# Attention loop of a decoder layer: values a step later, weight rounding off GpSimd, thresholds of the context spread out

## What is computed

```python
# attention input and its result ("context"), per chunk of 64 tokens:
ch_bias = (max + min) / 2 per channel;  xz = xp - ch_bias
tmax = max|xz| per chunk;  cmax = max|xz| per chunk and channel
thr = tmax / 2 ** arange(7, -1, -1);  idx = sum(cmax > thr[:7])
scale = tmax / 2 ** (7 - idx) / 7
result = clip(round(xz / scale), -8, 7) * scale
# attention
probs = softmax(Q K^T);  ctx = probs V
# ternary FFN weights
scale = mean|w|;  wq = clip(round(w / scale), -1, 1) * scale
```

## Time and profile before

| what | us |
|---|---|
| median of three runs | 1176.83 (1174.73 to 1180.32) |
| the profiled execution | 1178.66 |
| its span, first to last instruction | 1176.9 |
| first stage, to the first row maximum | about 128 |
| attention loop | about 510 |
| third stage | about 537 |

### The profile page before, as it was taken

The page is one execution under the profiler, slowest core; times in us unless marked ns, Lnnn a source line. Parts: engine busy times, 40 slices in busy tenths (PEclk is TensorE's granted clock), DMA queues, the critical chain, the costliest instruction groups (busy, mean ns, idle before and its releaser), DMA issues. The chain is left out here.

```text
span 1176.9 us, 13444 instructions
## 1 busy us (share of the span) xinstructions
PE 955.5 (81%) x4128; PEld 369.3 (31%) x4128; DVE 863.0 (73%) x1622; ACT 688.4 (58%) x1103; POOL 388.9 (33%) x303
## 2 busy tenths in 40 slices
PE   3667799889998888988887678797989798879465
PEld 1223322222222222222122343343434343434122
DVE  7996688888899989999883658568656765575245
ACT  3778377777777677767564034265526562555255
POOL 4103355656665676653002423130014001400000
PEclk9779699999999999999999879999999899989788
DMA  8966455555556554546334102310251025002500
GB/s 306 350 234 213 163 153 164 170 180 181 182 181 181 163 172 153 177 138 178 92 101 137 56 38 64 80 72 1 58 120 73 1 53 120 7 1 61 118 1 36
DMA packets 90684, 145.00 MB, mean 123 GB/s; under 512 B 12339, under 2 KB 52147, under 8 KB 89078
## 3 DMA queue, kind: packets, MB, share of 16 engines
q1 hardware_dynamic: 90614, 144.16, 40.7%
HBM read 84.75 MB, written 42.21 MB: 108 GB/s over the span
## 5 line engine op out<-in xcount | busy, mean ns | idle before, releaser
L1277 DVE TENSOR_REDUCE neg_max<-banks 128x1 f32<-128x512 f32 x512 | 331.4, 683 | 48.2 <-PE banks L1129 44.7
L1237 ACT ACTIVATE probs<-banks 128x512 f32<-128x512 f32 x512 | 278.3, 600 | 116.3 <-PE banks L1150 115.5
L1129 PE MATMUL banks<-k_st,q_st 96*128 96x512 bf16 x512 | 198.0, 392 | 20.9 <-DVE neg_max L1277 18.4
L1150 PE MATMUL banks<-q_st,k_st 99*128 99x512 bf16 x512 | 195.4, 385 | 13.2 <-ACT probs L1237 9.3
L1164 PE MATMUL banks<-probs,v_st 128*32 128x512 f32 x1024 | 137.1, 607 | 17.5 <-ACT pv_z L1250 16.3
L1543 POOL TENSOR_TENSOR rstd<-vare,half 128x1 f32<-128x1 f32 x48 | 26.8, 558 | 358.7 <-DVE vare L1535 358.7
L1749 PE MATMUL banks<-q_T,f_int_all 128*128 128x512 bf16 x512 | 127.5, 391 | 19.5 <-DVE h_ring L1770 19.4
L1129 PEld LDWEIGHTS banks<-k_st,q_st 96*128 96x128 bf16 x512 | 50.4, 99 | 171.2 <-DVE neg_max L1277 105.3
L1808 PE MATMUL banks<-hz,I_h 128*128 128x512 f32 x128 | 67.9, 667 | 34.5 <-DMA hz<-h_turned 32.1
L1759 DVE TENSOR_TENSOR h_ring<-banks,gate_row 128x512 f32<-128x512 f32 x64 | 44.1, 689 | 60.3 <-PE banks L1749 58.5
L1399 POOL TENSOR_SCALAR woT<-woT 128x1024 f32<-128x1024 f32 x24 | 87.2, 3633 | 2.4 <-ACT woT L1393 0.4
(11 more groups left out here) (263 smaller groups left out, 1519.1 us busy)
## 6 DMA issues: line engine op xcount, KB each, us to landing
hz<-h_turned SPq DMA_DIRECT2D x64, 256.0 KB
f_int_all<-in_ffn_dram SPq DMA_DIRECT2D x24, 512.0 KB, 8.6
qk_parts<-parts SPq DMA_DIRECT2D x32, 384.0 KB, 2.5
q_st<-qk_parts SPq DMA_DIRECT2D x32, 384.0 KB, 3.9
k_st<-qk_parts SPq DMA_DIRECT2D x32, 384.0 KB, 4.9
woT<-in_ffn_dram SPq DMA_DIRECT2D x24, 512.0 KB, 3.4
qk_parts<-parts SPq DMA_DIRECT2D x32, 256.0 KB, 2.9
pv_rows<-pv_z SPq DMA_DIRECT2D x32, 256.0 KB, 5.1
```

Source lines behind the costliest of these rows:

```text
L1129: pe.matmul(s_bank[(16 * g.n + tile) % SB], q_st[g.i][0:KR, j, qt * P:(qt + 1) * P], k_st[g.i][0:KR, j, :], start=True, stop=True).then_in ...
L1150: pe.matmul(st_bank[at % STB], k_st[g.i][:, j, kt * P:(kt + 1) * P], q_st[g.i][:, j, :], start=True, stop=True).then_inc(st_mm, 1)
L1237: act.activation(probs[ktp][:, j, i, :], st_bank[(16 * g.n + 2 * w + i) % STB], ACT.Exp).then_inc(exp_done, 2)
L1277: dve.tensor_reduce(neg_max[:, g.h, tile:tile + 1], s_bank[(16 * g.n + tile) % SB], AX.X, ALU.max, negate=True).then_inc(max_done, 1)
```

## The change

PV_AT goes from steps 1, 2, 6, 7 to 2, 3, 6, 7. An FFN piece is loaded second in SP's period rather than last, clipped by DVE in step 5 of its group (one instruction with two operations), and stored as bf16 by ACT in step 0 of the next group (an activation with bias -MAGIC); POOL has no part in it. The 11 threshold pieces go to steps 1, 3, 5, 7 of r = 0 and steps 1 to 7 of r = 1; POOL's scaling goes from r = 1 to r = 2; ACT's four roundings go from steps 1 to 4 to steps 1, 3, 5, 7 of r = 3; DVE's four finishing operations go from steps 5, 6, 7 of r = 3 and step 0 of r = 4 to step 7 of r = 3, step 0 of r = 4, and steps 1 and 6 of r = 5.

```diff
+        neg_magic = keep("neg_magic", [P, 1])
...
                 def _(pool):
+                    pool.memset(neg_magic[:], -MAGIC)
...
-            PV_AT, QK_AT, V_AT, HIGH_AT, MIDDLE_AT = (1, 2, 6, 7), (3, 5), 5, (4, 6), (5, 7)
+            N_AT = ((3, 7), (4, 0), (5, 1), (5, 6))
+            PV_AT, QK_AT, V_AT, HIGH_AT, MIDDLE_AT = (2, 3, 6, 7), (3, 5), 5, (4, 6), (5, 7)
             def v_bank(kt):
...
                             act_middle(act, g.tile(2), MIDDLE_AT.index(u))
-                    if g.b > 1 and g.r == 3 and 1 <= u <= 4:
-                        act_round(act, g.b - 2, u - 1)
+                    if g.b > 1 and g.r == 3 and u % 2:
+                        act_round(act, g.b - 2, u // 2)
+                    if u == 0 and 0 < g.n <= PIECES:
+                        act_ffn_store(act, g.n - 1)
...
+                    if u == 5 and g.n < PIECES:
+                        dve_ffn(dve, g.n)
             def dve_context(dve, g, u):
...
-                    else:
-                        dve_levels(dve, g.b - 2, u - 1)
-                if g.b > 1 and g.r == 1 and u < 4:
-                    dve_levels(dve, g.b - 2, 7 + u)
-                if g.b > 1 and g.r == 3 and u > 4:
-                    dve_n(dve, g.b - 2, u - 5)
-                if g.b > 1 and g.r == 4 and u == 0:
-                    dve_n(dve, g.b - 2, 3)
+                    if u % 2:
+                        dve_levels(dve, g.b - 2, u // 2)
+                if g.b > 1 and g.r == 1 and u:
+                    dve_levels(dve, g.b - 2, 3 + u)
+                if g.b > 1 and (g.r, u) in N_AT:
+                    dve_n(dve, g.b - 2, N_AT.index((g.r, u)))
...
-                if g.n < PIECES:
-                    pool_ffn(pool, g.n)
                 if g.b and g.r == 7:
-                if g.b > 1 and g.r == 1:
+                if g.b > 1 and g.r == 2:
...
             def sp_period(sp, g):
+                if g.n + 1 < PIECES:
+                    sp_ffn(sp, g.n + 1)
...
-                if g.n + 1 < PIECES:
-                    sp_ffn(sp, g.n + 1)
-                    need(sp, "f_done", 2 * PIECES)
+                    need(sp, "f_done", PIECES)
                     load_wo(sp, woT[:], bo_row[:])
             def sp_ffn(sp, c):
-                need(sp, "f_done", 2 * (c - 1))
+                need(sp, "f_done", c - 1)
             def act_ffn(act, c):
...
-            def pool_ffn(pool, c):
+            def dve_ffn(dve, c):
-                need(pool, "f_round", c + 1)
-                did(pool.tensor_scalar(raw, raw, MAGIC - 1.0, MAGIC + 1.0, ALU.max, ALU.min), "f_done")
-                need(pool, "f_done", 2 * c + 1)
-                did(pool.tensor_scalar(f_int_all[:, c, :], raw, -MAGIC, None, ALU.add), "f_done")
+                need(dve, "f_round", c + 1)
+                did(dve.tensor_scalar(raw, raw, MAGIC - 1.0, MAGIC + 1.0, ALU.max, ALU.min), "f_clip")
+            def act_ffn_store(act, c):
+                need(act, "f_clip", c + 1)
+                did(act.activation(f_int_all[:, c, :], f_ring[:, c % 2, :], ACT.Identity, bias=neg_magic[:]), "f_done")
             def groups(eng, period):
```

## The result

The changed kernel takes 1194.8 us, median of 4 runs, against 1178.6 for the kernel before on the same occasion: a ratio of 1.016 (95% interval 1.011 to 1.022). Forecast was 1164.1 in a range of 1152 to 1176. It is slower where a gain was forecast, and lies above the slower rival's 1187 too.

The account below looks back on a forecast made before the run. PE was taken to bound even groups, DVE and ACT to pace odd ones. Terms -3.5 - 3.4 + 5.5 - 3.8 - 1.4 - 3.2 - 1.0 - 1.4 - 0.5 gave -12.7, so 1164.1 us median, range 1152 to 1176.

Parts of the forecast that it names:

- slower rival: Store on ACT not hidden, 1.1 per even group, with the clip's 1.2; odd groups gain nothing: 1187 us, chance 0.08.
- PV a step later: Steps 1 to 3: PV's wait for pv_z goes; alone -0.5 us for an odd group, nothing for an even one.
- cost C of a plain even group: Net change per plain even group from PV's move, store and clip: +0.5 us, eleven groups +5.5.
- The store on ACT: Step 0, 24 times, ahead of step 1's exponentials: some 0.5 us in an even group, nothing in an odd one.
- the clip: DVE's step 5, 24 times: 0.6 us and a wait of about 0.5 in even groups; odd groups' lighter steps absorb it.
- a clock of 0.91: Group 19: gaps from roundings, a late piece and finishing operations give half speed for 3.4 us; spreading gives -3.2.
- Pieces off POOL, and sooner: About 0.4 us off a plain group's maxima chain; groups 5 and 7 return 1.2 and 0.5 each, -3.4 together.
- Thresholds spread: Groups 16 -2.9, 24 -2.6, 17 +0.9, 25 +0.8: net -3.8 us.
- Scaling, rounding and finishing: Group 18 -1.4 us, 19 -3.2, 27 -1.0, 14 and 22 -0.7 each, 26 to 30 in all -0.5.
- The wait in sp_spread: Group 21: SP waits until step 6 for finishing operations; store of values and sums behind it are needed later: nothing.
- The rule on the shared port: Exclusive lock for a whole instruction would give about 50 us off; the row gives 7 at most, and it decides.

Follow-up runs that it names:

- pv_only: The kernel before with only the values' multiplications moved to steps 2, 3, 6, 7: 1195.2 us, ratio 1.016.
- pv_fill: The kernel before with values in steps 2, 3, 6, 7, plus four unused matmuls on PE in step 1 ahead of the transpose: 1182.0 us, ratio 1.005.
- after_fill: The changed kernel with four unused matmuls added on PE in step 1: 1177.3 us, ratio 1.000.
- ffn_only: The kernel before with only the pieces changed (clipped by DVE, stored by ACT, loaded early): 1166.1 us, ratio 0.992.
- ctx_only: The kernel before with only the context's thresholds, scaling, rounding and finishing at their new steps: 1186.8 us, ratio 1.008.
- pv_back_n_early: The changed kernel with values back in steps 1, 2, 6, 7 and the last finishing operations earlier, at (4, 6) and (5, 1): 1165.0 us, ratio 0.991.
- ffn_clip7: The kernel before with only the pieces changed, and the clip in step 7 instead of 5 in groups 6, 14, 22: 1166.8 us, ratio 0.992.
- pv_split: The kernel before with values in steps 2, 4, 6, 7 of even groups and 2, 3, 6, 7 of odd ones: 1190.6 us, ratio 1.013.

## Why the prediction was wrong

*PV a step later* is the step that failed. I put it at "-0.5 for an odd group and at nothing for an even one". Alone it measured +19.7 us, 18.9 of them between the loop's first and last maximum. Three things were wrong in it, and one more in the cost C of a plain even group that it went into.
- I saw that the transpose would wait for DVE's last part and that step 3 would be 3.1 us, but charged neither. The wait went from 7.7 to 40.8 us; PV in step 1 had been the work that hid it. (In group 4 I also took the start of DVE's last part, 199.62, for its end, 199.79.) The late PV did slip into a gap of the odd groups: in pv_only's groups 9 and 11 step 3 grew by 1.1 and step 5 shrank by as much. But step 1 kept nearly all of its length, idle where PV had been, so they gained 0.3 and 0.2 us, not 0.5, and groups 3 and 13 lost 1.4 and 1.6 to the clock.
- Step 3 of an even group went up by the full 1.1 us of a PV, of which I had charged only a share, and "nothing" for the move alone. Steps 1 and 2 gave back 0.85 (I had 0.6): together +0.3 in pv_only's groups 2 and 4, and up to +1.4 in group 10, where DVE's last part comes later.
- TensorE's clock was in the sum only as a past gain ("a clock of 0.91" in group 19). That idle time at a new place could lose it was not among the terms nor the rivals. It is the largest: pv_fill gives back 13 of the 19.7 us and after_fill 17.
- The store on ACT costs 0.57 in steps 1 and 2 of the changed kernel's groups 2 and 4, near the 0.5 charged (in 8 to 12, where DVE's last part comes later, the waits for it cover most of that), and the clip, of which I had charged a share, costs nothing. So C, put at +0.5, measured +0.8 in groups 2, 4 and 8, +1.0 in 10 and +0.3 in 12: not far off, but from terms of which the largest, step 3, was mis-sized. The other even groups, from 6 to 22, add the clock, or stand among the terms below.

*The slower rival* had 0.08. Its mechanism, the store on ACT (1.16 us, 24 times) ahead of step 1's exponentials, is there, at half its price: 0.57 instead of 1.1, and only together with the values' move; in ffn_only the even groups stay at 14.6. Its clip of 1.2 costs nothing in the plain groups, its loss in the odd groups did not come, and the clock, which it did not have, brought more than both: that its 1187 lies nearest to 1194.8 is in part luck.

*Pieces off POOL, and sooner*: right in sign. Groups 5 and 7 returned 1.8 each (forecast 1.7), odd groups 0.6 to 0.7 (forecast 0.5). But the 0.5 was booked for PV's move and the pieces together and comes from the pieces: ffn_only alone gives 0.4 to 0.6. For each of groups 14 and 22 I forecast -0.7, and it is +3.8 and +3.5: I took GpSimd's relief into account there, not that the clip itself runs into GpSimd's subtraction (1.52), next to c_cmax which does the same.

*Thresholds spread*: 16 gained 2.8 alone (forecast 2.9) and 17 lost 1.5 (0.9). In the whole, 16 lost the gain to a wait of 2.52 for the maxima, to step 3 (4.3 us, PV with projection) and to a half clock, and 17 lost 3.1 with a double one.

*Scaling, rounding and finishing*: for group 19 I forecast -3.2 from spreading them. Without the values' move it did fall, to 15.5, but it does so in ffn_only too, where nothing of them is spread; spread alone, in ctx_only, it grew to 21.4. The gain was GpSimd's relief from the pieces, booked to the wrong part. In the whole it kept 1.0 of it, with a wait of 2.14 for the maxima and a half clock.

*The wait in sp_spread* was named and costed at "nothing", with "the store of values and the sums, needed a group later" behind it. What was left out is that the sums wait in turn for the store to land, about 5 us, and that the next group's maxima's DMA stands behind both: +5.1 in group 30, 8.5 in time in pv_back_n_early. At group 21 the same queue sent the maxima's row 1.5 after it was there (490.95 against 489.48), and that was still in time.

*The rule on the shared port*: the row decided rightly. L1290's like fell from 453 to 353 ns in ffn_only and to 202 in the changed kernel, so at most 32 x 0.25 = 8 us of DVE's time, nowhere near 50. In the trace before, the cast that ran into L1399 ended 1.06 after L1399's start in 17 groups, whether it had begun 0.47 or 0.66 after it; in the three groups where it began more than 1.5 after it, it took 0.16 to 0.20.

Left open: the store's 0.57 is read from the traces and was not tried by a run that leaves the store alone out; why some waits on PE have a half clock behind them and others of the same length have none; and why ffn_clip7's shorter groups didn't show in its time.

## What to carry to other kernels

Before moving work out of a wait, ask what it hides: the PV that waited 0.6 for its bank covered a longer wait for another engine in the same step (1.3 on average, 40.8 us in 31). An operation that is hidden where it stands, like the store here, may be hidden by the very work that is moved. Price a gap on PE by what the granted clock does behind it as well: here a gap of 1.8 us in a loop otherwise at full clock was followed by 3.4 us at half, and some ten such intervals were most of the loss. And when a wait is added to a queue, follow the queue for a whole period: the instruction that pays may be the third one behind it, in the next group.

## What was not expected of the hardware

That four matmuls whose results nobody reads make a kernel 13 us faster (granted clock 0.95 to 1.00), and 15 us slower where no gap is. That in pv_split the half clock returns in each odd group from 3 to 19 and in none of the even ones between (247.20 and 277.90 in the rows above). That the length of a wait alone doesn't decide it: in pv_only the transpose waited 1.92 or 1.93 us in seven odd groups, 3 to 13 and 21, and the half clock came behind it in 3, 13 and 21 only. And GpSimd's tensor_scalar of 3.63 us held VectorE only for about its first us, where its tensor_tensor held it to the end.
